# Last attention stage: rank and gate factors as f16 pairs instead of f32

## What is computed

```python
probs = softmax(xf @ Wg.T + bg)                      # 8 experts
top_w, top_idx = top_k(probs, 2)
combine = zeros(t, 8).at[rows, top_idx].add(top_w)   # the gates
h  = einsum('td,erd->ter', xf, A) + ba               # 8 experts x 16 ranks = 128
hw = h * combine[:, :, None]
delta = (einsum('ter,eor->to', hw, Bm) + combine @ bb) * 2
qkv = xf @ Wqkv.T + bqkv + delta
attn = softmax(q @ k.T * 64 ** -0.5)
out  = (attn @ v) @ Wproj.T + bproj
```

## Time and profile before

| | |
|---|---|
| time, median of 3 runs | 3629.27 us (3622.4 to 3633.48) |
| profiled execution: its own time | 3634.88 us |
| profiled execution: span | 3633.0 us, 61927 instructions |
| busy in the span | PE 3238.3 us (89%), PEld 2396.6 (66%), DVE 1780.8 (49%), POOL 1286.2 (35%), ACT 777.7 (21%) |
| mean granted TensorE clock | 0.955 |
| gate stretch (first pair starts) | to 2816.88 us |
| starts of the six pairs | 2816.88, 2937.03, 3060.10, 3182.20, 3302.30, 3425.04 us |
| final projection starts | 3549.46 us |

### The profile page before, as it was taken

The page is one execution under the profiler, slowest core; times in us unless marked ns, Lnnn a source line. Parts: engine busy times, 40 slices in busy tenths (PEclk is TensorE's granted clock), DMA queues, the critical chain, the costliest instruction groups (busy, mean ns, idle before and its releaser), DMA issues.

```text
span 3633.0 us, 61927 instructions
## 1 busy us (share of the span) xinstructions
PE 3238.3 (89%) x19394; PEld 2396.6 (66%) x19395; DVE 1780.8 (49%) x2943; ACT 777.7 (21%) x1106; POOL 1286.2 (35%) x1379
## 2 busy tenths in 40 slices
PE   6999999787786899998788788999986999999999
PEld 5788887666665788887666665776754555555555
DVE  6566666445444333333444444234378564556451
ACT  1211211000000221221000000444422335433540
POOL 2671112656554000002555654000042236523652
PEclk9999999999998999999889998999998999999999
DMA  4333343777766223233676766200041000000003
GB/s 140 106 132 116 122 140 124 242 229 250 237 217 203 70 93 115 92 117 128 218 227 224 249 224 224 81 13 26 13 125 51 18 18 18 15 4 18 18 8 108
DMA packets 101160, 433.83 MB, mean 119 GB/s; under 512 B 19647, under 2 KB 19970, under 8 KB 96817
## 3 DMA queue, kind: packets, MB, share of 16 engines
q0 software_dynamic: 55712, 266.87, 22.7%
q1 hardware_dynamic: 42593, 124.83, 10.8%
q10 hardware_dynamic: 2736, 40.50, 3.1%
HBM read 355.21 MB, written 76.88 MB: 119 GB/s over the span
## 4 chain that ended last, share of the span: by engine, by line
PE 65%; DVE 12%; DVEq 7%; issue 7%; another core or an unknown queue 6%; ACT 1%; POOL 1%; DMA 1%; POOLq 0%; SPq 0%; ACTq 0%
PE PS L1517 24%; PE PS L1647 12%; PE PS L1852 5%; PE PS L1680 3%; PE PS L1787 3%; PE PS L1526 3%; DVE NM L1438 2%; DVE HOT L1207 2%; DVEq L1207 2%; PE PS L1688 2%; PE PS L1835 2%; PE PS L1836 2%; PE PS L1725 1%; PE PS L1791 1%
## 5 line engine op out<-in xcount | busy, mean ns | idle before, releaser
L1517 PE MATMUL PS<-WHL,XT 128*125 (+1 forms) x3240 | 553.2, 330 | 16.3 <-issue 7.1
L1517 PE MATMUL PS<-WHL,HT 128*125 (+1 forms) x3240 | 536.6, 328 | 9.7 <-DVE ROOT L1166 8.6
L1517 PEld LDWEIGHTS PS<-WHL,XT 128*125 128x125 f16 (+1 forms) x3240 | 441.7, 138 | 104.0 <-issue 15.4
L1517 PEld LDWEIGHTS PS<-WHL,HT 128*125 (+1 forms) x3240 | 443.7, 137 | 96.5 <-DVE ROOT L1166 9.0
L1189 DVE SCALAR_TENSOR_TENSOR ROOT<-PS,GS,ROOT x182 | 185.2, 1018 | 526.7 <-remote 261.4
L618 POOL TENSOR_TENSOR PL<-PF 125x500 bf16<-125x500 f32 (+1 forms) x360 | 320.4, 925 | 277.4 <-ACT PF L825 274.6
L1647 PE MATMUL PS<-GATB,HOT 128*125 128x384 f16 x1440 | 290.7, 362 | 92.5 <-DVE HOT L1207 66.8
L1207 DVE SCALAR_TENSOR_TENSOR HOT<-NODE,DSTF,WHLO (+1 forms) x720 | 297.1, 474 | 78.4 <-issue 68.2
L1050 DVE SCALAR_TENSOR_TENSOR MSG<-PS,MSG 125x768 f16<-125x768 f32 x160 | 153.0, 956 | 361.9 <-ACT MSG L651 360.4
L1647 PEld LDWEIGHTS PS<-GATB,HOT 128*125 x1440 | 216.3, 152 | 165.1 <-issue 115.9
L1647 PE MATMUL PS<-ROW,HOT 128*125 128x384 f16 x1392 | 263.8, 348 | 60.1 <-DVE HOT L1207 40.7
(11 more groups left out here) (262 smaller groups left out, 4428.8 us busy)
## 6 DMA issues: line engine op xcount, KB each, us to landing
msg_table<-MSG SPq DMA_DIRECT2D x160, 336.0 KB
WST<-in_wg_dram ACTq DMA_DIRECT2D x16, 2304.0 KB
WST<-in_wf_dram SPq DMA_DIRECT2D x7, 1536.0 KB
KROW<-key_rows POOLq DMA_DIRECT2D x54, 192.0 KB, 3.8
msg_table<-MSG SPq DMA_DIRECT2D x160, 39.0 KB
WST<-in_wm_dram SPq DMA_DIRECT2D x5, 1152.0 KB
GATB<-msg_table,SKEY POOLq DMA_INDIRECT x216
ROW<-msg_table,SKEY POOLq DMA_INDIRECT x216
```

The source lines that it names most:

```text
L1517: ins = pe.matmul(PS[0:ROWS, b0 + h, 0:HALF], X[:, xp, k, bass.ts(t, ROWS)], panel_part(slot, wp, k, h), start=k == 0 and xp + wp == 0, st ...
```

## The change

- The two f32 blocks become f16 pairs. FH is the high part of both blocks and FL the low part of block 6; LTH and LTL are the same for the rows. Four f16 matmuls take the place of two f32 ones: FH·LTH, FH·LTL, FL·LTH for the ranks, and one of 96 rows for the gates. For that the gate rows of the panel are laid out three times (at rows 0, 32 and 64 of block 7), and HG's nine gate columns too, so that high·high, low·high and high·low come out of one product: rows 32 to 63 of FH hold the weights' low part, rows 64 to 95 of LTH the rows' low part.
- ACT makes FH ahead of the panel's high part (`split_ranks`); DVE makes FL and rows 32 to 63 of FH, in place of F67. The scales that this needs are made on POOL (`ffn_scales`, in place of `panel_scales`).
- The bound of HG is taken before the gates are applied: DVE's maximum over the ranks alone, the exponent, a PE transpose, DVE's maximum of the row, a PE broadcast, and six small DVE operations (`rank_top`, `rank_scales`). The queries' scale comes from the same bound; the f32 maximum over all of HG and POOL's all-reduce go.
- After the first panel's split DVE makes the low parts LTL and LTH[64:96] of the five transposed pieces out of PSUM. PE no longer waits for ACT's five copies before the first pair but for lt_low, ahead of the rank products of each chunk.
- The three fills of KX and V go to POOL, and PE waits for them ahead of the first score block.

```diff
@@ DVE, split_low (every pair)
-                    v.tensor_scalar(F67[:], WST[:, WM:WF], SC[:, WSCALE], None, ALU.mult)
-                    v.drain()
+                    v.scalar_tensor_tensor(FL[:, 0, :], WST[:, WM:WM + 3 * 128], RS[:, FSC], FH[:, 0, :], ALU.mult, ALU.subtract)
+                    v.scalar_tensor_tensor(FH[32:64, 1, :], WST[32:64, WM + 3 * 128:WF], RS[32:64, FSC], FH[32:64, 1, :], ALU.mult, ALU.subtract)
@@ ACT (first panel, and block 38 of every pair)
+            def split_ranks(q):
+                act.wait_ge(S["w_scale"], q + 1)
+                act.activation(FH[:].rearrange("p k c -> p (k c)"), WST[:, WM:WF], ACT.Copy, scale=RS[:, FSC])
+                split_high(q, W=WHM, cols=WM)
-                        split_high(it + (W_FFN + 1), W=WHM, cols=WM)
+                        split_ranks(it + (W_FFN + 1))
@@ POOL (first panel, and block 34 of every pair)
+            def ffn_scales():
+                g.tensor_scalar(SCI[:, WSCALE], SCI[:, POW], -1.0, float((254 + TOP) << 23), ALU.mult, ALU.add)
+                g.tensor_scalar(SC[:, XWINV], SC[:, POW], RS[:, UP], 2.0 ** -TOP / X_SCALE, ALU.mult, ALU.mult)
+                g.drain()
+                g.tensor_tensor(RS[:, FSC], SC[:, WSCALE], RS[:, RANKS], ALU.mult)
+                g.drain()
+                g.tensor_tensor(SC[:, WSCALE], SC[:, WSCALE], RS[:, DOWN], ALU.mult)
+                g.drain()
+                g.sem_inc(S["w_scale"], 1)
-            g.wait_ge(S["lt_max"], 1)
-            g.partition_all_reduce(QK[:, LALL], QK[:, LPOW], 128, bass.bass_isa.ReduceOp.max).then_inc(S["lt_pow"], 1)
+            g.wait_ge(S["rank_scale"], 1)
+            ffn_scales()
+            g.memset(KX[DH:DH + 1, :, :], SHIFT)
+            g.memset(V2[:, 0, :, :, 64:128], 1.0)
+            g.memset(V2[:, 1, :, :, 64:128], 0.0)
...
@@ DVE, gate stretch
+            v.tensor_reduce(RS[0:ROWS, RMAX], HG[:, :, 0:LW], AX.XY, ALU.max, apply_absolute_value=True)
+            v.tensor_scalar(RSI[0:ROWS, RPOW], RSI[0:ROWS, RMAX], EXPONENT, None, ALU.bitwise_and).then_inc(S["rank_top"], 1)
...
+            v.tensor_copy(HG[:, :, LW + 32:LW + 96].rearrange("p t (a c) -> p t a c", c=32)[:, :, :, 0:EXPERTS + 1],
+                          HG[:, :, LW:GATE].unsqueeze(2).broadcast_to([ROWS, RT, 2, EXPERTS + 1]))
...
-            v.tensor_reduce(QK[0:ROWS, LMAX], HG[:].rearrange("p t c -> p (t c)"), AX.X, ALU.max, apply_absolute_value=True)
-            v.tensor_scalar(QKI[:, LPOW], QKI[:, LMAX], EXPONENT, None, ALU.bitwise_and).then_inc(S["lt_max"], 1)
-            v.wait_ge(S["lt_pow"], 1)
+            for u in range(RT // 2):
+                v.wait_ge(S["lt_free"], u + 1)
+                v.scalar_tensor_tensor(LTL[:, rows], psum[:, 0, :], RS[:, LTS], LTH[:, 0, rows], ALU.mult, ALU.subtract)
+                v.scalar_tensor_tensor(LTH[64:96, 1, rows], psum[64:96, 1, :], RS[64:96, LTS], LTH[64:96, 1, rows], ALU.mult, ALU.subtract).then_inc(S["lt_low"], 1)
@@ PE
+            pe.wait_ge(S["rank_top"], 1)
+            pe.transpose(PS[0:1, 0, 0:128], RS[:, RPOW], IDF[:]).then_inc(S["rank_row"], 1)
+            pe.wait_ge(S["rank_one"], 1)
+            pe.matmul(PS[:, 0, 256:257], ONER[:], RTOP[:], start=True, stop=True).then_inc(S["rank_all"], 1)
-            pe.wait_ge(S["lt_free"], RT // 2)
-            pe.wait_ge(S["ffn_ready"], 1)
+                def ranks(x):
+                    c = slice(x * 128, (x + 1) * 128)
+                    return ((FH[:, 0, c], LTH[:, 0, :]), (FH[:, 0, c], LTL[:]), (FL[:, 0, c], LTH[:, 0, :]), (FH[0:96, 1, c], LTH[0:96, 1, :]))
-                        for k in range(2):
-                            ins = pe.matmul(PS[:, ffn.bank(f"{nm}{c}"), 0:n], ranks(k, x), LT[:, k, c0:c0 + n], start=False, stop=k == 1)
+                        if it == 0:
+                            pe.wait_ge(S["lt_low"], (2, 4, 5)[c])
+                        for n_, (weights, rows) in enumerate(ranks(x)):
+                            ins = pe.matmul(PS[:, ffn.bank(f"{nm}{c}"), 0:n], weights, rows[:, c0:c0 + n], start=False, stop=n_ == 3)
```

More of the change, by code:

```diff
@@ L110, in graph_and_attentions_kernel @@
         qctx = top.enter_context(ExitStack())
-        F67 = sb(qctx, "F67", [128, 2 * 3 * 128], f32)
+        FH = sb(qctx, "FH", [128, 2, 3 * 128], f16)
+        FL = sb(qctx, "FL", [128, 2, 3 * 128], f16)
         QS = sb(qctx, "QS", [128, 2, N], f16)
@@ L183, in graph_and_attentions_kernel @@
         fctx = ExitStack()
-        LT = sb(fctx, "LT", [128, 2, N], f32)
+        LTH = sb(fctx, "LTH", [128, 2, N], f16)
+        LTL = sb(fctx, "LTL", [128, N], f16)
+        RS = sb(fctx, "RS", [128, 8], f32)
+        RSI = RS[:].bitcast(i32)
+        ONER = sb(fctx, "ONER", [1, 128], f32)
+        RTOP = sb(fctx, "RTOP", [1, 1], f32)
+        RMAX, RPOW, RALL, LTS, RANKS, DOWN, UP, FSC = (slice(n_, n_ + 1) for n_ in range(8))
         HG = sb(fctx, "HG", [ROWS, RT, 256], f32)
@@ L306, in graph_and_attentions_kernel @@
         block = top.enter_context(nc.Block())
+        LT_BANK = (3, 4, 5, 7, 2)
+        GATE = LW + EXPERTS + 1
         def tview(b0):
@@ L779, in _ @@
             act.activation(GP[:, 1], GP[:, 0], ACT.Exp).then_inc(S["gate_ex"], 1)
-            split_high(W_FFN, W=WHM, cols=WM)
+            split_ranks(W_FFN)
             for u in range(RT // 2):
                 act.wait_ge(S["lt_pe"], u + 1)
-                act.activation(LT[:, :, 2 * u * ROWS:2 * (u + 1) * ROWS], PS[:, 2 + u, 0:4 * ROWS].rearrange("p (k c) -> p k c", k=2), ACT.Copy,
-                               scale=X_SCALE).then_inc(S["lt_free"], 1)
+                act.activation(LTH[:, :, 2 * u * ROWS:2 * (u + 1) * ROWS], PS[:, LT_BANK[u], 0:4 * ROWS].rearrange("p (k c) -> p k c", k=2), ACT.Copy,
+                               scale=RS[:, LTS]).then_inc(S["lt_free"], 1)
             act.wait_ge(S["qk_scale"], 1)
@@ L1348, in _ @@
             v.tensor_tensor(GP[:, 0], LOG, over(GM[:, 0, :]), ALU.subtract).then_inc(S["gate_in"], 1)
+            rank_top()
             v.wait_ge(S["gate_ex"], 1)
@@ L1784, in keys_or_queries @@
                         ffn.wait_banks(pe, it, f"{nm}{c}")
+                        if it == 0 and c == 2:
+                            pe.wait_ge(S["lt_low"], RT // 2)
                     for k in range(*part):
@@ L1808, in _ @@
                                 pe.matmul(o, XT[:, xp, k, t * ROWS:(t + 1) * ROWS], wf(wp, k, 2), start=k == 0 and wp + xp == 0, stop=False)
-                        for k in range(2):
-                            ins = pe.matmul(o, LT[:, k, t * ROWS:(t + 1) * ROWS], ranks(k, 2), start=False, stop=k == 1)
+                        for n_, (weights, rows) in enumerate(ranks(2)):
+                            ins = pe.matmul(o, rows[:, t * ROWS:(t + 1) * ROWS], weights, start=False, stop=n_ == 3)
                         if t % 4 == 3 or t == RT - 1:
@@ L1830, in _ @@
                         c0, n = CHUNKS[c]
+                        if it + h + c + t == 0:
+                            pe.wait_ge(S["ffn_ready"], 1)
                         if t == 0 and c == 0:
@@ L1901, in lay_out @@
     o["tri"] = np.tile(np.tril(np.ones((EXPERTS, EXPERTS), np.float32), -1).reshape(1, -1), (128, 1))
-    wf = np.concatenate([a["L0_ffn_Wqkv"].T, a["L0_ffn_Bm"].transpose(0, 2, 1).reshape(LW, 3 * D), a["L0_ffn_bb"],
-                         a["L0_ffn_bqkv"][None], np.zeros((128 - EXPERTS - 1, 3 * D), np.float32)])
+    gates = np.zeros((128, 3 * D), np.float32)
+    for r in (0, 32, 64):
+        gates[r:r + EXPERTS], gates[r + EXPERTS] = a["L0_ffn_bb"], a["L0_ffn_bqkv"]
+    wf = np.concatenate([a["L0_ffn_Wqkv"].T, a["L0_ffn_Bm"].transpose(0, 2, 1).reshape(LW, 3 * D), gates])
     o["wf"] = np.ascontiguousarray(wf.reshape(KF, 128, 3, PAIRS, 128).transpose(3, 1, 0, 2, 4)).reshape(PAIRS * 128, WF)
```

41 lines of the change are left out of this document (28 added, 13 removed).

## The result

The changed kernel takes 3616.51 us (median of 20 runs, 3606.8 to 3629.96) against 3632.26 us of the kernel before (20 runs beside them): a ratio of 0.9956 with a 95% interval of 0.9948 to 0.9965, by which it is 16.0 us less (12.7 to 18.9). The profiled execution took 3606.8 us, the least of the 20; its span is 3605.0, 28 us less than that of before. Of these, 8.3 us lie ahead of anything that the change touches: the last logit products start at 2789.97 us and not at 2798.31.

What follows compares the result with a forecast made beforehand. PE bounds a pair's start, DVE's maxima the M stage, POOL the S stage's second half. Pairs -27.7, S stage +7.2, gate stretch -0.2 and clock +2 give -18.7 us: 3629.27 to 3610.6 us, own range 3605 to 3617 (overall 3601 to 3622).

Steps and rivals of the forecast that it cites:

- q0 to M00: Start of a pair: q0, k0 and k1 save 0.84 us each, k2 about 0.15; together 2.65 us less.
- M stage: DVE's maxima hide W1 to W5; q1 gives 0.84 us and q2 0.43, together 1.27 us less per pair.
- To the scores: From the last maxima to the scores: R0 earlier and a shorter wait for W8 and W9, 0.7 us less.
- S stage: Added work delays POOL's stream: ACT's activation 0.75 us, DVE's two operations 0.45; 1.2 us more per pair.
- Gate stretch: Before the first pair: earlier DVE start against added rank operations; first pair starts 0.2 us earlier, bounds -1.5 and +3.
- The clock: Half-clock stretches in M stages, 2.0 us each in four pairs; first and fourth may get one too: 2 us more.
- Sum: Whole kernel: -27.7 + 7.2 - 0.2 + 2 = -18.7 us, from the median to 3610.6 us.
- the S stage takes much more (3619): Rival: POOL's scales outlast ACT's delay and DVE's operations cost their full 0.9 us; 2.65 us per pair, chance 0.13.
- nothing of it arrives (3603): Rival: POOL closes up, so the S stage's added work does not reach the pair's end; -26 us, chance 0.09.
- each pair gets two half-clock stretches (3624.6): Rival: two half-clock stretches in each pair's M stage, 16 us in place of 2; -4.7 us, chance 0.07.
- the clock falls throughout (3678): Rival: PE at 1.2 GHz all through the M stage, making the kernel slower at about 3678 us; chance 0.04.
- PE gains only half (3624): Rival: f16 products with 96 rows or a 125-column weight are slower than their neighbours, halving the gain; chance 0.05.

Runs made afterwards that it cites:

- a3: Changed kernel with the four rank products doubled in W1 to W5 and in k2: q0 to M00 19.84 us, M00 to R0 34.07 us.
- a4: Changed kernel with the four rank products doubled in q0 and the last part of q1: q0 to M00 20.53 us, M00 to R0 34.91 us.
- a1: Changed kernel without ACT's 768-column activation FH at block 38 of the six pairs: S stage 60.7 us, POOL's stream to block 38 36.40 us.
- g1: Changed kernel with POOL's three fills started only after DVE's fifth low part of LT: gate stretch 18.01 us, whole run 3609.9 us.
- b1: Kernel before, with ACT's high part at block 14 and DVE's F67 and low part after O01: S stage 58.26 us, run 3635.1 us.
- a2: Changed kernel without DVE's operations FL and FH after O10 of the six pairs: S stage 59.23 us.
- s2: Changed kernel with g1's late fills, ACT's split at block 14 and DVE's low parts after O01: 3598.68 us, ratio to the kernel before 0.9917.
- s5: Changed kernel with g1's late fills, ACT's split at block 14, DVE's FL and FH low part after O01, panel's low part after O10: ratio 0.9891.

## Why the prediction was right, by its steps

- **q0 to M00**, -2.65: measured -2.63, the third of k2's saving included, which a3 confirms with +0.16 for +0.43 of work.
- **M stage**, -1.27: -1.76 less the 2 x 0.26 of W6 and W7 is -1.24. The hidden W rows are hidden (a3), q1 is on the path in full (a4).
- **To the scores**, -0.7 with the two rows of values: 0.52 up to R0 and 0.31 behind it in pairs where the DMA is not late. In the second and fifth pair it is late in both kernels (R0 to the scores 4.2 us in the changed kernel, 4.1 and 3.8 before), and at most the 0.52 arrives.
- **S stage**, +1.2: +1.16. Of the mechanisms both are shown. The step of ACT at block 38 was taken as 0.75, and is 0.83. POOL's four scale operations, put at nothing since ACT's delay hides them, are hidden: without it they would cost 0.12 (a1). The wait that they had to be hidden in was read from the rows as 0.26 us in one place and 0.29 in another; 0.29 is right. The step of DVE's two operations was taken as 0.45 and is 0.32. F67 had contended with POOL too: in the trace of before one part beside it took 1.33 us. The Trainium skill (GPSIMD Engine Reference, Specifications), which has two-port modes contend as well as two inputs, pointed the right way from the 0.45; whether F67 ran in such a mode no trace here tells.
- **Gate stretch**, -0.2: wrong, 0.9 us more at equal clock and 1.5 between the first two profiles. The step that failed is the fills at no cost on POOL. I had the mechanism as a bound of +3 ("if POOL's fills and scales slow DVE beside them") and gave it no value; g1 shows 2 us of it.
- **The clock**, +2: not borne out. The first profile has 1.3 us less of it than before, the second 0.7 less, and that both other pairs drop as well did not occur: M stages hit are two and four, against four and five before. No single wait of PE shortly ahead of these falls is longer than 0.66 us, in either kernel. What I had not seen is a second place, the end of the S stage, 1.4 us each in one or two pairs. That PE's longer wait for POOL there brings it about is not shown. The kernels in which that wait is 1.3 us or less (before, b1, a2, s2 to s5) have no fall there; a1, with 1.74 us, has it in all six pairs; with 2.04 us it is two pairs and one in the changed kernel's two profiles, one in g1 and in a3, none in a4.
- **Sum**: -6 x 3.54 + 1.5 without disturbances is -19.7 us, the profiles from the touched part on show -19.6 and -20.6, the prediction -18.7. Two errors, the gate stretch (1.1 to 1.7 us too low) and the clock (2.7 to 3.3 us too high), cancel in part, and that is luck. The profiled execution was to take 3616.2 us and took 3606.8; most of the difference, 8.3 us, stands ahead of the change. The medians show -16.0 (-12.7 to -18.9). That the last three or four microseconds between the profiles and the medians are lost in the untouched part or in disturbances that two profiles don't show is open; no run tells it.
- **Rivals**: that the S stage takes much more (3619), that nothing of it arrives (3603), that each pair gets two half-clock stretches (3624.6), that the clock falls throughout (3678) and that PE gains only half (3624) did not occur. The first has its mechanism in small, the second became true only in s5, with its S stage of 58.28 us under the 58.70 of before.

## What to carry to other kernels

Halve the work of a step where another engine waits for it and the saving arrives to the hundredth of a microsecond; elsewhere it is free to give away. Price the preparation of it as carefully: an activation and two small vector operations beside the engine that paces a stage cost a quarter of the gain here, and all of it came back when they were moved apart, each to a place where the pacing engine had work in hand and had caught up. A fill moved to an idle engine is not free if it holds up the engine it was taken from: here the fills on POOL cost DVE 2 us.

## What the runs showed of the hardware that was not expected

- A POOL memset of 2500 columns on one partition (2.17 us) held a DVE tensor_scalar of 80 f32 columns from 0.20 to 1.53 us, and one of 1280 columns a copy from 0.26 to 0.94; DVE's operations with two tensors read, right beside them, kept their length (0.24 us). In the other direction a POOL tensor_scalar on one column took 1.55 us in place of 0.26 beside DVE's 640-column operations.
- Beside DVE's f32 and f16 split of 2304 columns a POOL part took 3.33 us in place of 1.02; beside the operations of 384 columns, one on 128 partitions and one on 32, two parts in a row took 1.33 each. F67, with one tensor read and 768 columns, cost POOL the same 0.31.
- A wait of 2.04 us of PE for POOL was followed by a stretch at half clock in 5 of 30 pairs (the changed kernel's two profiles, g1, a3, a4), one of 1.74 us in 6 of 6 (a1), and one of 1.3 us or less in none of 48. So the length of the wait alone does not tell.
